# Decay projection and router logits computed by four column groups of TensorE, with the logits placed between two halves of the gate projection

## What is computed

```
kg     = x @ Wkg1.T @ Wkg2.T + bkg2     # decay: 512 -> 16 -> 256
gproj  = x @ Wg.T + bg                  # gate, 512 -> 512
gk     = log_sigmoid(kg) / 16
logits = x3 @ Wgate + bgate             # router: 512 -> 4, in float32
top_vals, top_idx = top_k(logits, 2)
```

## Time and profile before

| | us |
|---|---|
| median of 3 runs | 1058.67 |
| lowest, highest | 1053.78, 1058.72 |
| profiled execution, its own time | 1052.63 |
| its span on the core | 1050.9 |
| PE busy | 932.2 (89% of the span) |
| DVE busy | 697.7 |
| POOL busy | 499.1 |
| ACT busy | 453.1 |
| one full turn of the pipeline | 34.18 |

### The profile page before, as it was taken

How to read it: one execution, slowest core, us unless ns; L and a number is a source line. 1 busy time by engine, 2 the same in 40 slices (tenths; PEclk the granted TensorE clock), 3 DMA queues, 4 the chain that set the end, 5 groups by cost and what they waited for, 6 DMA issues and landing times.

```text
span 1050.9 us, 19085 instructions
## 1 busy us (share of the span) xinstructions
PE 932.2 (89%) x7297; PEld 559.8 (53%) x7297; DVE 697.7 (66%) x1293; ACT 453.1 (43%) x754; POOL 499.1 (47%) x563
## 2 busy tenths in 40 slices
PE   3688999999999999999999663069999999999995
PEld 1446666766666766776676442034444444444342
DVE  6767677878887788778886545856554445345672
ACT  3444555565566655665555423122232333233210
POOL 1447677767677777767775720111070001003643
PEclk9788999999999999999999965569999999999998
DMA  8413000000000000000000006032335234335593
GB/s 289 133 51 128 4 15 18 5 17 17 15 2 17 17 14 14 6 17 14 17 2 14 11 12 229 26 115 83 118 90 191 80 121 160 100 100 198 159 243 121
DMA packets 40300, 78.39 MB, mean 75 GB/s; under 512 B 11378, under 2 KB 11650, under 8 KB 40258
## 3 DMA queue, kind: packets, MB, share of 16 engines
q1 hardware_dynamic: 35266, 63.13, 18.0%
q0 software_dynamic: 4992, 14.70, 5.1%
HBM read 64.16 MB, written 13.65 MB: 74 GB/s over the span
## 4 chain that ended last, share of the span: by engine, by line
PE 74%; DVE 7%; POOL 5%; issue 4%; DMA 4%; SPq 3%; ACT 1%; POOLq 0%; DVEq 0%; ACTq 0%
PE ps L1009 18%; PE ps L1010 17%; PE ps L1011 17%; PE ps L1015 6%; PE ps L1102 4%; PE ps L1181 3%; PE ps L1197 3%; POOL y_fetched L728 2%; PE ps L1206 2%; POOL hrs L596 2%; PE ps L1226 2%; DVE big L1674 1%; DMA y_fetched<-y_scratch,idx_get 1%; SPq L473 1%; PE ps L1114 1%
## 5 line engine op out<-in xcount | busy, mean ns | idle before, releaser
L596 POOL TENSOR_TENSOR hrs<-hve,neg_half 128x16 f32<-128x16 f32 x48 | 140.2, 2921 | 3.8
L982 ACT ACTIVATE big<-ps 128x512 f32<-128x512 f32 x64 | 38.2, 597 | 233.2 <-PE ps L1011 233.0
L1771 DVE TENSOR_SCALAR big<-big 128x512 f16<-128x512 f32 x64 | 27.8, 435 | 110.4 <-ACT big L982 110.3
L1009 PE MATMUL ps<-w2h,big 128*128 128x512 f16 x256 | 97.0, 379 | 2.5 <-DVE big L1363 2.5
L1009 PE MATMUL ps<-big,w1h 128*128 128x512 f16 x256 | 97.8, 382 | 1.4 <-DVE big L1363 1.4
L1011 PE MATMUL ps<-big,w1l 128*128 128x512 f16 x256 | 97.8, 382 | 0.0
L1010 PE MATMUL ps<-big,w1h 128*128 128x512 f16 x256 | 97.8, 382 | 0.0
L1010 PE MATMUL ps<-w2l,big 128*128 128x512 f16 x256 | 97.0, 379 | 0.0
L1011 PE MATMUL ps<-w2h,big 128*128 128x512 f16 x256 | 97.0, 379 | 0.0
L711 POOL DMA_INDIRECT big<-x_scratch,token_of x16 | 18.3, 1147 | 149.3 <-PE ps L1015 77.5
L728 POOL DMA_INDIRECT y_fetched<-y_scratch,idx_get x32 | 37.5, 1173 | 104.8 <-DMA y_scratch<-big 89.4
(11 more groups left out here) (305 smaller groups left out, 2530.5 us busy)
## 6 DMA issues: line engine op xcount, KB each, us to landing
wst<-in_w SPq DMA_DIRECT2D x28, 1024.0 KB, 5.2
x_scratch<-xn SPq DMA_DIRECT2D x16, 256.0 KB, 2.1
y_fetched<-in_w SPq DMA_DIRECT2D x4, 1024.0 KB, 13.4
out<-x_all SPq DMA_DIRECT2D x4, 1024.0 KB, 7.9
pr<-in_w_attn SPq DMA_DIRECT2D x3, 1024.0 KB, 8.4
x_all<-in_w_attn SPq DMA_DIRECT2D x3, 1024.0 KB, 11.7
x_all<-in_x SPq DMA_DIRECT2D x1, 3072.0 KB, 11.7
y_scratch<-big SPq DMA_DIRECT2D x3, 1024.0 KB, 6.1
```

Source lines behind the costliest of these rows:

```text
L596: pool.tensor_tensor(hrs[n][:, :], hve[n][:, :], neg_half[:, :], ALU.pow).then_inc(hdev[n], 1)
L982: act.activation(hg[f % 2], psum[f % 2][:, 512:1024], ACT.Gelu, scale=UN).then_inc(hg_r, 1)
L1009: nc.tensor.matmul(o, lh, rh, start=first, stop=False)
```

## The change

The decay's first projection writes each chunk's product to its own 32 partitions of PSUM (partitions 32k to 32k+31, the array's column group k), in the order high x high for all chunks, low x high for all, high x low for all. So the four chunks' partial sums lie side by side in `kg1` (now 128 rows). `wkg2_sb` holds `w_kg2` four times, at rows 32k, so the second matmul, now over 128 rows, adds the partial sums. The row of ones is made by the bias operand of ACT's copy. Stationary tiles are padded with zeros to 32 columns.

The router's logits change operands: the padded 128 x 32 weight is stationary, the chunk of `x3T` moves, and the four products go to four column groups. ACT copies these partial sums to `lgT`, and one more float32 matmul with `sum_e` (a matrix of ones at 32k+e, e) adds them, tokens on partitions. The four logits matmuls stand between two halves of `a1_g`; the summing matmul takes the old place at the turn's end.

ACT's order: `x3_out` ahead of the second norm, `parts_out` behind it. SP: three more loads in `consts_a1`, all of which wait for five fills on DVE. POOL: three more fills and selects for constants at the start.

```diff
-        wkg2_sb = sb("wkg2_sb", [DK + 1, QK])
+        wkg1h = sb("wkg1h", [P, KC, 32], F16)
+        wkg1l = sb("wkg1l", [P, KC, 32], F16)
+        wkg2_sb = sb("wkg2_sb", [P, QK])
...
-        consts_a1 = [..., (wkg2_sb[0:DK, :], w_kg2), ...]
+        consts_a1 = [..., *[(wkg2_sb[32 * k:32 * k + DK, :], w_kg2) for k in range(KC)], ...]
...
+            sp.wait_ge(dve_const, 1)
...
-                take(kg1[0:DK, :], a1[0:DK, 0:L], UN, kg1_r)
+                act.activation(kg1[:, :], a1[:, 0:L], ACT.Identity, scale=UN, bias=kg_one[:, :]).then_inc(kg1_r, 1)
...
+            def parts_out(s):
+                b, par, half = s
+                after(act, x3_ps, b, nth=2, per=3)
+                take(lgT[:, :], d1[:, 0:L], 1.0, x3T_r)
...
                 on(s[1], kv_out)
+                on(s[3], x3_out)
                 on(s[1], row_norm, 1, xn2, xn2_r)
+                on(s[3], parts_out)
                 on(s[0], ctx_hi)
-                on(s[3], x3_out)
                 on(s[1], x2_hi)
                 on(s[3], logits_out)
...
-                for k in range(KC):
-                    last = mm3(a1[0:DK, 0:L], wh[:, k, C_KG:C_KG + DK], wl[:, k, C_KG:C_KG + DK],
-                               xth[:, k, :], xtl[:, k, :], k == 0, k == KC - 1)
+                products = ((wkg1h, xth), (wkg1h, xtl), (wkg1l, xth))
+                for n, (w, xt) in enumerate(products):
+                    for k in range(KC):
+                        last = nc.tensor.matmul(a1[32 * k:32 * k + 32, 0:L], w[:, k, :], xt[:, k, :],
+                                                start=n == 0, stop=n == len(products) - 1)
...
-                    last = nc.tensor.matmul(d1[:, 0:E], x3T[:, k, :], wgate_sb[:, k, :], start=k == 0, stop=k == KC - 1)
+                    last = nc.tensor.matmul(d1[32 * k:32 * k + 32, 0:L], wgate_sb[:, k, :], x3T[:, k, :], start=True, stop=True)
...
+            def b2_logits_sum(s):
...
+                after(pe, x3T_r, s[0], nth=2, per=2)
+                nc.tensor.matmul(d1[:, L:L + E], lgT[:, :], sum_e[:, :], start=True, stop=True).then_inc(x3_ps, 1)
...
-                on(s[0], a1_g)
+                on(s[0], a1_g, range(KC // 2))
+                on(s[3], b2_logits)
+                on(s[0], a1_g, range(KC // 2, KC))
                 on(s[1], b1_x)
-                on(s[3], b2_logits)
+                on(s[3], b2_logits_sum)
...
+            dve.memset(wgate_sb[:, :, :], 0.0)
+            dve.memset(wkg1h[:, :, DK:32], 0.0)
+            dve.memset(wkg1l[:, :, DK:32], 0.0)
+            dve.memset(carry[:, :], 1.0)
+            dve.memset(wkg2_sb[:, :], 0.0).then_inc(dve_const, 1)
```

More of the change, by code:

```diff
@@ L104, in decoder_layer @@
         cent_sums = sb("cent_sums", [P, KC, HEADS])
-        wgate_sb = sb("wgate_sb", [P, KC, E])
+        wgate_sb = sb("wgate_sb", [P, KC, 32])
+        lgT = sb("lgT", [P, L])
+        sum_e = sb("sum_e", [P, E])
         row_id = sb("row_id", [P, 1], I32)
@@ L571, in _ @@
             pool.wait_ge(pool_const, 4)
+            pool.affine_select(out=kg_one[:, :], in_=kg_one[:, :], compare_op=ALU.not_equal, fill=1.0, base=-DK,
+                               pattern=[[0, 1]], channel_multiplier=1).then_inc(pool_const, 1)
             pool.affine_select(out=ident[:, :], in_=ident[:, :], compare_op=ALU.not_equal, fill=1.0, base=0,
@@ L575, in _ @@
                                pattern=[[0, 2], [1, L]], channel_multiplier=-1).then_inc(pool_const, 1)
+            for k in range(KC):
+                pool.wait_ge(pool_const, 7 + k)
+                pool.affine_select(out=sum_e[:, :], in_=sum_e[:, :], compare_op=ALU.not_equal, fill=1.0, base=-32 * k,
+                                   pattern=[[-1, E]], channel_multiplier=1).then_inc(pool_const, 1)
             def deviation(s, n):
@@ L766, in weights_attention @@
                 act.wait_ge(consts_a1_in, 16 * len(consts_a1))
-                act.activation(wh[:, :, C_KG:C_KG + DK], KG_STAGE, ACT.Copy, scale=WS).then_inc(stage_hi, 1)
+                act.activation(wkg1h[:, :, 0:DK], KG_STAGE, ACT.Copy, scale=WS).then_inc(stage_hi, 1)
             def second_hi():
@@ L796, in kg1_out @@
                 after(act, kg1_ps, s[0])
-                take(kg1[0:DK, :], a1[0:DK, 0:L], UN, kg1_r)
+                if first(s[0], 0):
+                    act.wait_ge(pool_const, 5)
+                act.activation(kg1[:, :], a1[:, 0:L], ACT.Identity, scale=UN, bias=kg_one[:, :]).then_inc(kg1_r, 1)
                 if first(s[0], 0):
@@ L918, in x3_out @@
             def x3_out(s):
-                after(act, x3_ps, s[0], nth=1, per=2)
+                after(act, x3_ps, s[0], nth=1, per=3)
                 take(x3T[:, :, :], cols(d1), 1.0, x3T_r)
+            def parts_out(s):
+                b, par, half = s
+                after(act, x3_ps, b, nth=2, per=3)
+                take(lgT[:, :], d1[:, 0:L], 1.0, x3T_r)
             def logits_out(s):
                 b, par, half = s
-                after(act, x3_ps, b, nth=2, per=2)
-                act.activation(logit_all[:, bass.ds(b * E, E)], d1[:, 0:E], ACT.Copy).then_inc(lg_r, 1)
+                after(act, x3_ps, b, nth=3, per=3)
+                act.activation(logit_all[:, bass.ds(b * E, E)], d1[:, L:L + E], ACT.Copy).then_inc(lg_r, 1)
             def body(s):
@@ L1016, in turn, with rows @@
                 last.then_inc(done, 1)
-            def rows(ps, xh, xl, col, done, opens=True):
-                for k in range(KC):
+            def rows(ps, xh, xl, col, done, opens=True, ks=range(KC)):
+                for k in ks:
                     last = mm3(ps, xh[:, k, :], xl[:, k, :], wh[:, k, col:col + D], wl[:, k, col:col + D], opens and k == 0, k == KC - 1)
-                last.then_inc(done, 1)
+                if k == KC - 1:
+                    last.then_inc(done, 1)
             def second_kv():
@@ L1087, in a1_g @@
                 after(pe, v_r, b)
-                rows(a1, xth, xtl, C_G, g_ps)
+                rows(a1, xth, xtl, C_G, g_ps, ks=ks)
             def a2_scores(s, rnd):
@@ L1223, in b2_logits @@
                     pe.wait_ge(consts_b_in, 16 * len(consts_b))
-                after(pe, x3T_r, b)
+                after(pe, x3T_r, b, nth=1, per=2)
                 for k in range(KC):
-                    last = nc.tensor.matmul(d1[:, 0:E], x3T[:, k, :], wgate_sb[:, k, :], start=k == 0, stop=k == KC - 1)
+                    last = nc.tensor.matmul(d1[32 * k:32 * k + 32, 0:L], wgate_sb[:, k, :], x3T[:, k, :], start=True, stop=True)
                 last.then_inc(x3_ps, 1)
+            def b2_logits_sum(s):
+                if first(s[0], 0):
+                    pe.wait_ge(pool_const, 7 + KC)
+                after(pe, x3T_r, s[0], nth=2, per=2)
+                nc.tensor.matmul(d1[:, L:L + E], lgT[:, :], sum_e[:, :], start=True, stop=True).then_inc(x3_ps, 1)
             def body(s):
@@ L1393, in weights_attention @@
                 dve.wait_ge(stage_hi, 1)
-                low(wl[:, :, C_KG:C_KG + DK], KG_STAGE, WS, wh[:, :, C_KG:C_KG + DK]).then_inc(stage_lo, 1)
+                low(wkg1l[:, :, 0:DK], KG_STAGE, WS, wkg1h[:, :, 0:DK]).then_inc(stage_lo, 1)
                 dve.wait_ge(dve_const, 6)
```

19 lines of the change are left out of this document (10 added, 9 removed).

## The result

| | before | changed |
|---|---|---|
| median of 20 runs each, us | 1058.38 | 1055.28 |
| lowest, highest | 1053.78, 1060.76 | 1049.33, 1058.42 |
| ratio of the two, 95% interval | | 0.9964 (0.995 to 0.9978) |
| profiled execution, its own time | 1052.63 | 1056.73 |
| its span | 1050.9 | 1055.0 |

The change makes the kernel 0.2 to 0.5% faster, 3.1 us by the medians: inside the 0.5% that the prediction called no change, and 2.3 us above its 1053. The two profiled executions alone would say the opposite (1055.0 against 1050.9). So the work starts with finding the piece of the trace that both kernels can be compared in.

A forecast was written before the change was run, and what follows sets the result against it. The prediction took PE to bound the full turns. Its terms, -5.0 + 0.3 + 2.1 - 0.4 + 0.5 = -2.5 us, put on a base of 1055.65, gave 1053; the range was about 1044 to about 1061.

The forecast's parts named there:

- the insertion: Logits matmuls between the gate projection's halves: +0.40 us a turn on PE, bounds 0.26 and +1.0.
- End of turn: From `b1_x` to the next scores: 1.61 us falls to 0.68, so -0.93 for PE.
- How much arrives before a2_o: From the turn's end to a2_o: only 0.70 of the 0.93 us can be won, as mask and kraw are late next.
- The decay's projection: The decay's twelve first-projection matmuls in column groups: 0.77 us falls to 0.53, -0.24, bounds -0.45 and 0.
- What of it arrives: Before qraw's transposes: both savings together give at most 0.82 us a turn, since PE needs qraw.
- The slower rival: No overlap at the insertion: +1.0 us there, 1059 on the profile or 1062 on the base; chance 0.10.
- The second projection and the rest of the turn: The 128-row second projection: 0, bounds -0.1 and +0.15 us; qraw's transposes to `b1_x`: unchanged.
- A full turn: One full turn of the pipeline: -0.82 + 0.40 = -0.42 us; twelve turns, 4 to 15, give -5.0.
- The start: SP's first list: three more loads +1.5, waiting for five fills +0.6, sum +2.1 us, bounds 0.6 and 3.
- Turn 1: The decay's twelve matmuls in turn 1, 1.38 us: groups take off about a full turn's share, -0.4 us.
- Turn 16: The tail: ACT's `x3_out` comes ahead of the norm that PE waits for, +0.5 us.
- The rival of a shorter chain: Chain outside PE gives PE all its 0.93 + 0.24: a turn -0.77, total 1043 to 1049 us; chance 0.20.

The follow-up runs named there:

- e8: The changed kernel with its summing matmul at the turn's end issued four times; ratio 1.0011 to before, turn 34.06 us.
- e5: The changed kernel with its eight logits records between the gate's halves issued twice; ratio 0.9985 to before, turn 34.08 us.
- e6: The kernel before profiled once more, nothing changed; span 1050.2 us, turn 34.19 us.
- e4: The changed kernel with DVE's order changed, the first norm's statistics and the heads' variance earlier; ratio 0.9882 to before, turn 33.39 us.
- e1: The kernel before with only the decay's projection by column groups, logits as before; ratio 0.9993, turn 33.89 us.
- e2b: The kernel before with only the router's logits changed, decay's projection as before; ratio 0.9933, turn 33.95 us.
- e3: The changed kernel with the second decay weight's copies and bias loaded by ACT instead of SP, same semaphore; ratio 1.0018 to before, turn 33.86 us.
- e7: e4 with the second decay weight's copies and bias loaded by ACT under a semaphore of their own; ratio 0.9877 to before, turn 33.39 us.

## Why the prediction came out as it did

The forecast of 1053 and of no change beyond 0.5% held, and with it the reason: of what PE saves a turn, the chain DVE, POOL, DVE lets 0.82 through by the forecast and 0.77 by the trace, and the insertion takes half of that or more back. Two things were luck. The forecast changed 1055.65, 2.7 below the median of before over 20 runs (1058.38), and the change came out at -3.1 instead of -2.5. And the errors of the terms below partly cancel. By its steps:

- *End of turn:* 0.68 forecast, 0.65 measured. *How much arrives before a2_o:* 0.70 forecast from the turn without logits, 0.68 measured. That turn was worth reading, as it showed the chain alone.
- *The decay's projection:* 0.24 forecast, 0.48 measured where nothing holds PE (e8), a little more than the forecast's own bound of 0.45. The 32 ns a matmul, read from float32 records, were the wrong price: the twelve float16 matmuls take 0.13 us to the last one's start. *What of it arrives,* 0.12 forecast, 0.09 measured. Since the chain holds the transposes, a price wrong by half did no harm. PE's own saving is thus 1.44 us a turn and not 1.17.
- *The insertion:* 0.40 forecast, 0.45 measured (e5: 0.22 records, 0.23 edges). The slower rival, one record after another for 1.0, did not happen.
- *The second projection and the rest of the turn:* 0 forecast, and the distance from qraw's transposes to the next `b1_x`, less the insertion, is 21.66 against 21.64.
- *A full turn:* -0.42 forecast, -0.32 measured; twelve of them -3.8 instead of -5.0. Three terms off by 0.02 to 0.05 each, all on one side.
- *The start:* +2.1 forecast, +1.5 measured. The fills and loads cost SP 1.7 (the piece issued at 29.72 now goes at 31.41). The fills were smaller than taken: SP's first dependent load goes at 1.74 instead of 1.28, 0.46 and not 0.6, and the four loads take 1.89 of SP together. The piece that landed at 38.08 now lands at 39.60, near the 40 that was forecast.
- *Turn 1:* the term most wrong in proportion, -0.4 forecast, -1.1 measured. The 1.38 us to the transposes became 0.43, at a granted clock of 0.50. That is a share of 0.69, and in a full turn it is 0.63 (0.77 to 0.28, e8): the rule that the share is the same held roughly, and what failed is the share, 0.31, which came from the price of 32 ns. The other 0.14 is in the transposes behind, 1.05 and now 0.91 to the second projection.
- *Turn 16:* +0.5 forecast. The stretch in question did lengthen by 0.49 (third norm's transposes to `b1_x` 1.64 before, 2.13 after). What the sum left out is that turn 16 begins with the saved end of turn 15: from there to qraw's transposes it takes 11.15 instead of 12.10 (e6). Together they leave -0.46, and 1.4 us between two executions of the changed kernel (33.05 and 31.63 for this turn) hide it.
- *No term at all:* the granted clock. It made one turn of before 1.6 us longer, and the likely cause of turns 1 and 2 being 0.6 and the drain 3.7 worse in the changed profile is the clock too. By the terms measured, +1.5 - 1.1 + 0.4 - 3.8 - 0.5, the change is -3.5; with the clock's pieces the spans of the two profiles of either kernel say anything between +5 and -7.

PE's waits are the two that were named, though only one shows as a wait. The rival of a shorter chain (-0.77 a turn) was wrong for this change and comes near what e4 makes of it (-0.79), though with a larger saving of PE and two small waits.

**Open.** Low-clock full turns, with PE busy all the time, came in 3 of 36 turns of kernels with the old logits at the turn's end (before, e1, e6) and in none of 108 of the kernels without them. e8, which has four-column matmuls for 0.9 us there again, had none in 12, and e6, from which at least one was expected if the old logits bring them on, had none either. So the old logits are not shown to bring them on, and I can't say what does. Nor is it settled why e2b's total is better than its turn.

## What to carry to other kernels

When a change takes work off the engine that bounds the loop, look for a turn of the same trace in which that work is missing, for it shows the chain that will be late next; here it gave the arriving part to 0.02 us. Two savings in front of the same wait don't add, so reorder the chain (here two of DVE's steps) before or with them: that took a gain of 0.4 to 0.6% to one of 0.8 to 1.2%. When the noted waits are gone, compare the start of each step with the end of what it reads: a distance that is the same in every turn (here 0.05 behind ACT's `pT`) is the next bound. And a small load on another queue shares the DMA engines, and one of single elements is slow there: give it a semaphore that only its own reader waits for.

## What the runs showed of the hardware

- Float16 matmuls of 128x32 by 128 columns in four column groups: the three sets of four start 0.065 us apart (328.58, 328.65, 328.71), so 16 ns a matmul and 0.28 us from the first to the transposes behind (e8). The Trainium skill (TensorE: Matmul & The Clock Gate, Wait — 56ns, not 53.3ns?) has a least distance of about 25 ns between starts; these are below it. Float32 records in groups cost 28 ns each (e5).
- A held step of PE starts 0.05 us after the other engine has written what it reads: the transposes 0.055 after DVE's `qraw` (changed, e1, e4, e8) and `b2_pv` 0.053 after ACT's `pT` (e1, e4, e8), the same within 0.002 in all eleven turns. A wait of 0.05 to 0.14 us had no note in the timeline, so a step that seems to cost more (transposes of 0.71 and 0.77 instead of 0.58) can be one that is held.
- 256 elements of four bytes, loaded through ACT's queue beside large pieces on SP's, kept their semaphore open until 18.9 us (e3) and 19.8 (e7); in SP's queue ahead of these pieces they are through by 8 (changed).
- `hrs`, a power of 128x16 values, takes POOL 2.92 us; the second of the pair took 3.24 to 3.25 where it follows the first within 0.3 us (changed, e2b, e3, e5, e8) and 2.92 where it stands further off (before, e1, e4), and no run says why.
- The granted clock was 0.64 and 0.79 in pieces of full turns with PE busy 3.00 of 3.00 us, so part of each ran at 1.2 GHz; in the 3 us ahead of them PE was busy 2.91 us at a granted clock of 1.00. In e1 it was 0.50 over 524 to 527, PE busy 3.00 of 3.00 us.
